# One top-p selection kernel: the repeat round is kept once per selection, and its ten halvings become a loop

## The chip, the core and the metric

The kernel is one program for one core of a Trainium2 chip. The metric is the device time of one execution in microseconds (us); lower is better. Three executions of the kernel before took 2766.83, 2774.76 and 2774.62 us, median 2774.62, mean 2772.07.

## The reference

The model is layer norm(x + G0), and then layer norm(x + G1) of that, on 3327 nodes with 128 features and a 3327 x 3327 adjacency matrix with values in 0.05 to 1 where there is an edge. G0 is a graph network with top-p ("nucleus") attention, in two steps:

```python
q = X @ W1.T @ W2.T ;  k = X @ W3.T
probs = softmax(q @ k.T)
idx = argsort(-probs) ; sp = take_along_axis(probs, idx) ; cs = cumsum(sp)
mask = ones where cs - sp < 0.9, at idx      # the largest until they hold 0.9 of the mass
A = probs * mask ; A = A / A.sum(-1)
# twice:  Xf = R @ Xf ; Xa = A @ Xa ; Z += Xf @ U1[n].T + Xa @ U2[n].T      R: adj + I, rows normalised
```

G1 has an edge part (a GRU cell on adj @ h, three graph attention heads with a masked softmax over every row) and a node part (a second GRU cell). The change concerns only G0, and in it only the step that decides which entries of a row of probabilities are kept.

## The kernel before

**Tiling.** 3327 rows are 26 tiles of 128 partitions, handled as 13 pairs (`PAIRS`). A row of logits or probabilities is 3328 wide and lies in a buffer `e`. `layer0` runs the two steps (step 0 and step 1), `normalize_and_sum` the norm and the sparse product, and a third function the attention heads (called layer 1 here).

**Who does what.** TensorE (PE) makes the logits (L819), the small transposes of flags (L861), the transposes of the kept probabilities (L925) with the products after them (L935), the adjacency product (L839) and the products `taken` (L879). ScalarE (ACT) copies and exponentiates, GpSimd (POOL) marks rows, SyncE (SP) issues the loads. VectorE (DVE) finds each row's largest values (L71), solves for the cut by halvings (the search, whose first instruction is L1304), and selects. The engines run streams of their own and meet at semaphores.

**The selection.** `Search.select` is placed twice for each pair, once for each of its two tiles `k`. Its inner function `divide` marks candidates of a tie at the cut (L439, a match-and-replace over the whole row), drops ties that exceed the mass (L444, the same kind of instruction), and keeps what is above the cut (L450). Between L439 and L444 stands an `If` (L480) on a register `kind`: where `kind` says OPEN, the search did not close the cut, and `another_round` narrows it. Between L444 and L450 stands a second `If` (L492) for more than 8 ties. Below, the part inside the first `If` is called the skipped body, since it is passed whenever `kind` is not OPEN.

**The skipped body.** It holds `another_round` twice: in `Fori(0, 3)` under an `If`, and in `while_over`, three nested loops of `Fori` and `If` (L80 to L86). Each `another_round` has ten halvings written out, one after another, each with a masked sum over the candidates of the round, a comparison with the wanted mass and a step up or down of the bit pattern `round_mid`. `while_over` places its body once, whatever its number of turns.

**Order of the work in step 1.** On DVE, `over_pairs_with_rows` is a loop of three turns with two pairs each (pairs 0 to 5), pair 6 written out, a loop of two turns (pairs 7 to 10), and pairs 11 and 12 written out; then comes `taken_batch`, one more tile with the rows that were taken out. A pair on DVE is: search of pair p, tops of pair p+1 for both tiles (L71), `assign_slots` (waits for PE's transposed flags), a wait for POOL, select of tile 0, select of tile 1. Each selection ends with a reciprocal (L1352) that lets PE start on that tile (L925). PE's loop is cut elsewhere, pairs 0 to 3 and 7 to 10; in a pair it does the transposes and products of both tiles, makes the logits two pairs ahead, and waits for the search of the next pair (L861). SP's `adj` loads run beside it, 1664 KB each. In step 0 a pair has no drops (L444) and no `adj` loads; a selection there first keeps (L450) and then passes the whole of `divide`, with the skipped body in it, by one jump, and the order is search, flags (L1340), select tile 0, tops, select tile 1, tops.

**What a text of the program does to an engine.** Each `select` is written out at each of its places in the instruction stream: a pair in a loop has two places, used by every turn. DVE has 21 selections placed; the skipped body stands in each.

Of the kernel before, what the change touches and what calls it, by code (L numbers as in the profile page):

```python
# [8 lines left out]
ALU = mybir.AluOpType  # L9
ACT = mybir.ActivationFunctionType  # L10
AX = mybir.AxisListType
# [7 lines left out]
ROUND_HALVINGS = 10  # L19
FINE_HALVINGS = 16  # L20
LOW_BITS = 0x37C00000
FIRST_STEP = 1 << 26
# [5 lines left out]
OPEN = 256  # L28
# [16 lines left out]
def spread_flags(eng, works):  # L45

    eng.drain()
    for w in works:
        eng.transpose(w["flags_t"][:, :], w["flags"][:, :])
    eng.drain()  # L50
    for w in works:
        eng.tensor_reduce(w["flag_max"][:, :], w["flags_t"][:, :], AX.X, ALU.max)
    eng.drain()
    for w in works:
        eng.tensor_copy(w["flag_int"][:, :], w["flag_max"][:, :])
    eng.drain()


def load_flag(eng, w, flag, regs):

    for q in range(4):
        eng.reg_load(regs[q], w["flag_int"][32 * q:32 * q + 1, 0:1])
    eng.reg_alu(flag, regs[0], regs[1], ALU.max)
    eng.reg_alu(flag, flag, regs[2], ALU.max)
    eng.reg_alu(flag, flag, regs[3], ALU.max)
# [8 lines left out]
def while_over(eng, flag, least, times, body):  # L74


    side = 1
    while side ** 3 < times:
        side += 1
    with eng.If(eng.snap(flag) > least):  # L80
        with eng.Fori(0, side):
            with eng.If(eng.snap(flag) > least):
                with eng.Fori(0, side):
                    with eng.If(eng.snap(flag) > least):
                        with eng.Fori(0, side):
                            with eng.If(eng.snap(flag) > least):  # L86
                                body()


class Search:  # L90
# [2 lines left out]
             "over", "up", "known", "reaches", "covers", "partial", "short", "strict", "backward", "cut_dropped", "scale", "levels", "shut", "mass_hi", "rowmax",  # L93
             "negmax", "open", "over_full", "spilled", "slot", "blank", "inv_kept0", "inv_kept1", "kept",
             "r_above0", "r_theta", "r_below", "r_was", "r_stays", "r_moves", "r_tau", "r_hi", "r_value", "r_bound",
             "r_above", "r_known", "r_up", "r_mass")

    def __init__(self, sb, width):
        self.width = width
# [32 lines left out]
    def one(self, name, k):  # L132
        return self.scalars[:, self.NAMES.index(name), k:k + 1]
# [194 lines left out]
    def another_round(self, eng, k, e):  # L328


        def one(name):
            return self.one(name, k)
# [18 lines left out]
        eng.memset(self.round_mid[:, :], LOW_BITS + FIRST_STEP)  # L351
        eng.drain()
        eng.tensor_tensor(one("r_stays"), one("r_stays"), one("known"), ALU.max)
        step = FIRST_STEP
        for n in range(ROUND_HALVINGS):
            eng.scalar_tensor_tensor(spare, cand, self.round_mid[:, :].bitcast(F32), cand, ALU.is_ge, ALU.mult,
                                     accum_out=self.mass[:, n, k:k + 1])
            back = -(step // 2) if n + 1 < ROUND_HALVINGS else 0
            eng.tensor_scalar(self.round_back[:, :], self.round_mid[:, :], float(back), None, ALU.add)
            eng.drain()  # L360
            eng.tensor_tensor(one("r_up"), self.mass[:, n, k:k + 1], one("r_theta"), ALU.is_ge)
            eng.drain()
            eng.scalar_tensor_tensor(self.round_mid[:, :], one("r_up"), float(step), self.round_back[:, :],
                                     ALU.mult, ALU.add)
            eng.drain()
            step //= 2
        eng.tensor_scalar(self.low[:, 0:ROUND_HALVINGS, k], self.mass[:, 0:ROUND_HALVINGS, k], one("r_theta"), None, ALU.is_lt)
        eng.drain()
        eng.tensor_tensor(self.low[:, 0:ROUND_HALVINGS, k], self.low[:, 0:ROUND_HALVINGS, k], self.mass[:, 0:ROUND_HALVINGS, k], ALU.mult)
        eng.drain()  # L370
        eng.tensor_reduce(one("r_hi"), self.low[:, 0:ROUND_HALVINGS, k], AX.X, ALU.max)
        eng.scalar_tensor_tensor(spare, cand, self.round_mid[:, :].bitcast(F32), cand, ALU.is_lt, ALU.mult)
        eng.drain()
        eng.max(top8, spare)
# [78 lines left out]
    def select(self, eng, k, e_pad, kind, flag, regs, both_ways, found=False):  # L453


        def another():
            self.another_round(eng, k, e_pad[:, 0:self.width])
            spread_flags(eng, [self.round])
            load_flag(eng, self.round, flag, regs)

        def more_ties():
            self.find_ties(eng, k)
            for n in range(TIES // 8):
                self.mark_ties(eng, k, n, self.work[:, :])
                eng.drain()
            self.pass_ties(eng, k)
            eng.tensor_scalar(self.one("r_up", k), self.one("left", k), 0.0, 4.0, ALU.is_gt, ALU.mult)
            eng.drain()
            eng.tensor_tensor(self.round["flags"][:, 0:1], self.one("r_up", k), self.one("strict", k), ALU.mult)
            spread_flags(eng, [self.round])  # L470
            load_flag(eng, self.round, flag, regs)

        def divide():
            if not found:
                if both_ways:
                    self.find_drops(eng, k)
                self.find_ties(eng, k)
            self.mark_ties(eng, k, 0, e_pad)
            eng.reg_mov(flag, kind)
            with eng.If(eng.snap(kind) > OPEN - 1):  # L480
                eng.drain()
                with eng.Fori(0, 3):
                    with eng.If(eng.snap(flag) > OPEN - 1):
                        another()
                while_over(eng, flag, OPEN - 1, self.width // 8, another)
                eng.drain()
                self.find_ties(eng, k)
                self.mark_ties(eng, k, 0, e_pad)
            eng.drain()
            if both_ways:  # L490
                self.drop_ties(eng, k)
            with eng.If(eng.snap(flag) > 1):  # L492
                eng.drain()
                self.mark_ties(eng, k, 1, self.work[:, :])
                with eng.If(eng.snap(flag) > 2):
                    eng.drain()
                    self.mark_ties(eng, k, 2, self.work[:, :])
                    eng.drain()
                    self.pass_ties(eng, k)
                    while_over(eng, flag, 3, self.width // TIES, more_ties)  # L500
                    eng.drain()
                eng.drain()
            eng.drain()
            self.keep(eng, k, e_pad, self.work)

        if both_ways:
            with eng.If(eng.snap(kind) > 0):
                divide()
            with eng.If(eng.snap(kind) < 1):
                self.keep(eng, k, e_pad, e_pad)  # L510
        else:
            with eng.If(eng.snap(kind) < 1):
                self.keep(eng, k, e_pad, e_pad)
            with eng.If(eng.snap(kind) > 0):
                divide()
        eng.drain()
# [1825 lines left out]
```

## Time and profile before

| | |
|---|---|
| span of the profiled execution | 2769.2 us |
| its own time | 2770.99 us |
| what lies outside the span | 1.8 us |
| runs | 2766.83, 2774.76, 2774.62 us |
| granted TensorE clock, mean | 0.934 of full speed |
| PE busy | 2355.1 us (85%), 17759 matmuls |
| DVE busy | 2199.7 us (79%), 6636 instructions |
| ACT busy | 1072.5 us (39%) |
| POOL busy | 141.5 us (5%) |

How to read it: busy time is summed over the whole span, in which stages with different limits follow each other. Step 0 of G0 is at about 67 to 510 us, step 1 at about 577 to 1458 us with `taken_batch` behind it, layer 1's attention from about 1600 us to the end. Idle time stands in brackets behind an instruction, with what ended it; "issue" is idle time in which the engine waited for nothing that the profile shows.

### The profile page before, as it was taken

Reading aid. Unit: us, or ns where it says so; the run is one execution under the profiler, and the core shown is the slowest. Engines: PE = TensorE matmul, PEld = TensorE weight load, DVE = VectorE, ACT = ScalarE, POOL = GpSimd, SP = SyncE. Lnnn points to the kernel's source line nnn. Section 1 sums busy time; section 2 is a strip of 40 time slices with the busy share of each in tenths; the row PEclk is TensorE's granted clock in tenths of the full one; section 3 lists DMA queues with packets and bytes.
Section 4 is the critical chain, followed back from the end, with each engine's and each line's share of the span. In section 5 each row is a group of like instructions: output and inputs, shape, how many; then the busy total and the mean of one; then the engine's idle time right before and its main releaser. Section 6 shows DMA issues by size and latency. Waiting matters only on the chain. (4 is left out here: it accounts for less than half of the span.)

```text
span 2769.2 us, 53551 instructions
## 1 busy us (share of the span) xinstructions
PE 2355.1 (85%) x17759; PEld 1987.9 (72%) x17759; DVE 2199.7 (79%) x6636; ACT 1072.5 (39%) x1785; POOL 141.5 (5%) x353
## 2 busy tenths in 40 slices
PE   5899998777888887888886649996999999999985
PEld 1566666555767776777775549995999999999952
DVE  2777777279888888888889777766999999999836
ACT  4566666433333333333333130003343443434423
POOL 0000000101111110000000010000000000000000
PEclk9999999997999998999997869998999999999997
DMA  3000000020222221222220235543334343433220
GB/s 128 2 2 1 1 1 2 1 89 17 95 100 100 100 100 51 100 100 101 100 100 14 87 128 202 202 164 127 126 108 143 101 146 104 141 110 134 94 88 25
DMA packets 57106, 245.00 MB, mean 88 GB/s; under 512 B 6705, under 2 KB 18352, under 8 KB 43120
## 3 DMA queue, kind: packets, MB, share of 16 engines
q1 hardware_dynamic: 56816, 241.94, 24.9%
q14 instruction: 207, 1.70, 0.2%
q8 instruction: 83, 1.36, 0.2%
HBM read 235.10 MB, written 6.82 MB: 87 GB/s over the span
## 5 line engine op out<-in xcount | busy, mean ns | idle before, releaser
L1932 PE MATMUL a_acc<-H,pT 128*128 128x128 f32 x4056 | 547.8, 277 | 11.7 <-ACT a_rows L1964 3.8
L1932 PEld LDWEIGHTS a_acc<-H,pT 128*128 128x128 f32 x4056 | 495.3, 192 | 28.7 <-DVE pT L2066 19.9
L935 PE MATMUL small<-XR,wT 128*128 128x128 f32 x2756 | 375.9, 282 | 28.3 <-ACT wT L1131 27.5
L71 DVE MAX8 cand<-e 128x8 f32<-128x64 f32 (+3 forms) x1898 | 302.7, 240 | 101.4 <-issue 101.2
L819 PE MATMUL lg<-kT,qs 128*128 128x512 f32 (+1 forms) x742 | 339.9, 596 | 50.5 <-ACT e L1075 38.5
L935 PEld LDWEIGHTS small<-XR,wT 128*128 128x128 f32 x2756 | 341.6, 196 | 44.4 <-ACT wT L1131 44.4
L2066 DVE TENSOR_TENSOR pT<-a_tr,a_adjT 128x512 f32<-128x512 f32 (+1 forms) x546 | 316.3, 643 | 22.5 <-PE a_tr L1891 19.3
L839 PE MATMUL accR<-XR,adj 128*128 128x129 f32 x2704 | 327.2, 283 | 0.0
L839 PEld LDWEIGHTS accR<-XR,adj 128*128 128x128 f32 x2704 | 324.1, 200 | 0.0
L1891 PE MATMUL a_tr<-ident,prob 128*128 128x128 f32 x2028 | 311.2, 274 | 10.9 <-ACTq L1958 10.9
L1131 ACT ACTIVATE wT<-tr 128x512 f32<-128x512 f32 (+1 forms) x371 | 206.2, 566 | 273.1 <-PE tr L925 271.4
L2044 DVE CUSTOM_DVE_ANT_0 prob<-a_adj,EB 128x3328 f32<-128x3328 f32 x78 | 282.6, 3623 | 0.0
L819 PEld LDWEIGHTS lg<-kT,qs 128*128 128x128 f32 x742 | 119.0, 193 | 216.9 <-ACT e L1075 168.6
L925 PE MATMUL tr<-ident,e 128*128 128x128 f32 x1378 | 213.2, 282 | 56.0 <-DVE scalars L1352 49.9
L1075 ACT ACTIVATE e<-lg 128x512 f32<-128x512 f32 (+1 forms) x371 | 206.3, 566 | 119.2 <-PE lg L819 117.3
L1891 PEld LDWEIGHTS a_tr<-ident,prob 128*128 128x128 f32 x2028 | 241.0, 142 | 11.1 <-issue 11.1
L1956 ACT ACTIVATE prob<-prob,a_negmax 128x3328 f32<-128x3328 f32 x78 | 239.0, 3064 | 9.1 <-DVE a_negmax L2053 9.1
L925 PEld LDWEIGHTS tr<-ident,e 128*128 128x128 f32 x1378 | 167.7, 146 | 95.7 <-DVE scalars L1352 51.6
L1580 PE MATMUL g_sp<-g_adj,H 128*128 128x128 f32 x1352 | 166.1, 286 | 17.1 <-ACTq L1645 17.1
L1580 PEld LDWEIGHTS g_sp<-g_adj,H 128*128 128x128 f32 x1352 | 161.9, 201 | 18.8 <-issue 18.2
L1085 ACT ACTIVATE e<-e,scalars 128x3327 f32<-128x3327 f32 x53 | 162.1, 3060 | 15.9 <-DVE scalars L1416 8.8
L219 DVE SCALAR_TENSOR_TENSOR work<-cand,mid 128x416 f32<-128x416 f32 (+1 forms) x198 | 143.2, 757 | 8.1
(334 smaller groups left out, 2457.1 us busy)
## 6 DMA issues: line engine op xcount, KB each, us to landing
adj<-in_adjT SPq DMA_DIRECT2D x52, 1664.0 KB, 7.3
g_adj<-in_adjT SPq DMA_DIRECT2D x26, 1664.0 KB, 6.9
a_adj<-in_adj SPq DMA_DIRECT2D x26, 1664.0 KB, 6.8
a_adjT<-in_adjT SPq DMA_DIRECT2D x156, 256.0 KB, 3.9
a_adjT<-in_adjT SPq DMA_DIRECT2D x26, 128.0 KB, 4.2
XT<-in_x_t SPq DMA_DIRECT2D x1, 1664.0 KB, 13.5
hT_scratch<-hT SPq DMA_DIRECT2D x1, 1664.0 KB, 12.2
nsT_scratch<-nsT SPq DMA_DIRECT2D x1, 1664.0 KB, 5.8
```

The source lines that it names most:

```text
L71: eng.max(cand[:, n, :], src[:, n * seg:min((n + 1) * seg, width)])
L819: eng.matmul(lg[bank][:, 0:sl.stop - sl.start], qs[k][:, :], kT[:, sl], start=True, stop=True).then_inc(lg_ready, 1)
L839: mm = eng.matmul(accR[:, :], adj[k][:, j * P:(j + 1) * P], xf[:, j, :], start=False, stop=(j == T - 1))
L925: mm = eng.transpose(tr[(k * NC + c) % 2][:, o:o + P], e[b][k][:, j * P:(j + 1) * P], ident[:, :])
L935: mm = eng.matmul(accA[:, :], wT[(k * NC + c - 1) % 2][:, o:o + P], xa[:, j, 0:P], start=(j == 0), stop=(j == T - 1))
L1075: eng.activation(e[b][k][:, sl], lg[chunk(step, 0, k, c) % 2][:, 0:sl.stop - sl.start], ACT.Copy).then_inc(lg_free, 1)
L1580: mm = eng.matmul(sp[k][:, :], H[:, j, :], adj[q][:, j * P:(j + 1) * P], start=(j == 0), stop=(j == T - 1))
L1891: mm = eng.transpose(tr[g % BANKS][:, (j % 4) * P:(j % 4 + 1) * P], prob[order[n][1]][:, j * P:(j + 1) * P], ident[:, :])
L1932: mm = eng.matmul(acc[:, :], pT[g % RING][:, (j % 4) * P:(j % 4 + 1) * P], H[:, j, :], start=(j == 0), stop=(j == T - 1))
L1956: eng.activation(prob[h][:, :], prob[h][:, :], ACT.Exp, bias=negmax[h][:, :], accum_out=den[h][:, :])
L2044: eng.tensor_tensor_reduce(prob[h][:, :], adj[k][:, :], EB[:, h, :], 1.0, -3.0e38, ALU.add, ALU.max, mx[h][:, :])
L2066: eng.tensor_tensor(pT[g % RING][:, 0:width(c)], tr[g % BANKS][:, 0:width(c)], adjT[:, c * 512:c * 512 + width(c)], ALU.mult).then_inc(pT_ ...
```

## The change

In `another_round` the ten halvings become `Fori(0, ROUND_HALVINGS)`. The step, a number of the program text before, is a value `r_step` that is halved in each turn, and the largest mass below the wanted one is kept as a running maximum `r_hi` instead of being taken from ten stored masses at the end; one addition behind the loop makes up for the last step. In `select` the `Fori(0, 3)` copy of the round goes, and only the one in `while_over` stays. While the three-turn loop and the nested loops both ran as long as the flag said OPEN, now the nested loops alone do.

```diff
--- before.py
+++ after.py
@@ -93,7 +93,7 @@
              "over", "up", "known", "reaches", "covers", "partial", "short", "strict", "backward", "cut_dropped", "scale", "levels", "shut", "mass_hi", "rowmax",
              "negmax", "open", "over_full", "spilled", "slot", "blank", "inv_kept0", "inv_kept1", "kept",
              "r_above0", "r_theta", "r_below", "r_was", "r_stays", "r_moves", "r_tau", "r_hi", "r_value", "r_bound",
-             "r_above", "r_known", "r_up", "r_mass")
+             "r_above", "r_known", "r_up", "r_mass", "r_step", "r_half", "r_low")
 
     def __init__(self, sb, width):
         self.width = width
@@ -351,24 +351,26 @@
         eng.memset(self.round_mid[:, :], LOW_BITS + FIRST_STEP)
         eng.drain()
         eng.tensor_tensor(one("r_stays"), one("r_stays"), one("known"), ALU.max)
-        step = FIRST_STEP
-        for n in range(ROUND_HALVINGS):
+        eng.memset(one("r_hi"), 0.0)
+        eng.memset(one("r_step"), float(FIRST_STEP))
+        eng.drain()
+        with eng.Fori(0, ROUND_HALVINGS):
             eng.scalar_tensor_tensor(spare, cand, self.round_mid[:, :].bitcast(F32), cand, ALU.is_ge, ALU.mult,
-                                     accum_out=self.mass[:, n, k:k + 1])
-            back = -(step // 2) if n + 1 < ROUND_HALVINGS else 0
-            eng.tensor_scalar(self.round_back[:, :], self.round_mid[:, :], float(back), None, ALU.add)
+                                     accum_out=one("r_mass"))
+            eng.tensor_scalar(one("r_half"), one("r_step"), 0.5, None, ALU.mult)
             eng.drain()
-            eng.tensor_tensor(one("r_up"), self.mass[:, n, k:k + 1], one("r_theta"), ALU.is_ge)
+            eng.tensor_tensor(one("r_up"), one("r_mass"), one("r_theta"), ALU.is_ge)
+            eng.scalar_tensor_tensor(one("r_low"), one("r_mass"), one("r_theta"), one("r_mass"), ALU.is_lt, ALU.mult)
+            eng.tensor_tensor(self.round_back[:, :], self.round_mid[:, :], one("r_half"), ALU.subtract)
             eng.drain()
-            eng.scalar_tensor_tensor(self.round_mid[:, :], one("r_up"), float(step), self.round_back[:, :],
+            eng.scalar_tensor_tensor(self.round_mid[:, :], one("r_up"), one("r_step"), self.round_back[:, :],
                                      ALU.mult, ALU.add)
+            eng.tensor_tensor(one("r_hi"), one("r_hi"), one("r_low"), ALU.max)
             eng.drain()
-            step //= 2
-        eng.tensor_scalar(self.low[:, 0:ROUND_HALVINGS, k], self.mass[:, 0:ROUND_HALVINGS, k], one("r_theta"), None, ALU.is_lt)
-        eng.drain()
-        eng.tensor_tensor(self.low[:, 0:ROUND_HALVINGS, k], self.low[:, 0:ROUND_HALVINGS, k], self.mass[:, 0:ROUND_HALVINGS, k], ALU.mult)
-        eng.drain()
-        eng.tensor_reduce(one("r_hi"), self.low[:, 0:ROUND_HALVINGS, k], AX.X, ALU.max)
+            eng.tensor_copy(one("r_step"), one("r_half"))
+            eng.drain()
+        eng.tensor_scalar(self.round_mid[:, :], self.round_mid[:, :], float(FIRST_STEP >> ROUND_HALVINGS), None, ALU.add)
+        eng.drain()
         eng.scalar_tensor_tensor(spare, cand, self.round_mid[:, :].bitcast(F32), cand, ALU.is_lt, ALU.mult)
         eng.drain()
         eng.max(top8, spare)
@@ -479,9 +481,6 @@
             eng.reg_mov(flag, kind)
             with eng.If(eng.snap(kind) > OPEN - 1):
                 eng.drain()
-                with eng.Fori(0, 3):
-                    with eng.If(eng.snap(flag) > OPEN - 1):
-                        another()
                 while_over(eng, flag, OPEN - 1, self.width // 8, another)
                 eng.drain()
                 self.find_ties(eng, k)
```

PE's, ACT's, POOL's and SP's streams keep every instruction and its order. DVE's stream gets shorter: 6869 rows before, 4286 after.

The first place is DVE's stream in the first selection of step 1, where the skipped body begins. `L439`/`L441` is the first mark of ties on the row `e`; the branches behind it are the `If` on `kind` and the loops; `L338` begins `another_round`. Before:

```order
L439 MATCH_REPLACE work<-hits,e 128x3336
L479 ISA
L480 COMPARE_AND_BRANCH
L482 UNCONDITIONAL_BRANCH
L483 COMPARE_AND_BRANCH
L338 SCALAR_TENSOR_TENSOR work,scalars<-e,scalars 128x3328
```

After:

```order
L441 MATCH_REPLACE work<-hits,e 128x3336
L481 ISA
L482 COMPARE_AND_BRANCH
L80 COMPARE_AND_BRANCH
L81 UNCONDITIONAL_BRANCH
L82 COMPARE_AND_BRANCH
L83 UNCONDITIONAL_BRANCH
L84 COMPARE_AND_BRANCH
L85 UNCONDITIONAL_BRANCH
L86 COMPARE_AND_BRANCH
L338 SCALAR_TENSOR_TENSOR work,scalars<-e,scalars 128x3328
```

Nothing ahead of the `If` has moved; behind it the first copy of the round is gone and the nested loops come at once.

The second place is inside `another_round` on DVE, the halvings on the candidates `round_cand`. One of ten halvings before:

```order
L356 SCALAR_TENSOR_TENSOR work,mass<-round_cand,round_mid 128x208
L359 TENSOR_SCALAR round_back<-round_mid 128x1
L361 TENSOR_TENSOR scalars<-mass,scalars 128x1
L363 SCALAR_TENSOR_TENSOR round_mid<-scalars,round_back 128x1
```

The whole loop after:

```order
L357 UNCONDITIONAL_BRANCH
L358 SCALAR_TENSOR_TENSOR work,scalars<-round_cand,round_mid 128x208
L360 TENSOR_SCALAR scalars<-scalars 128x1
L362 TENSOR_TENSOR scalars<-scalars 128x1
L363 SCALAR_TENSOR_TENSOR scalars<-scalars 128x1
L364 TENSOR_TENSOR round_back<-round_mid,scalars 128x1
L366 SCALAR_TENSOR_TENSOR round_mid<-scalars,round_back 128x1
L368 TENSOR_TENSOR scalars<-scalars 128x1
L370 COPY scalars<-scalars 128x1
L357 REGISTER_ALU
L357 COMPARE_AND_BRANCH
```

Forty instructions in each copy of the round have become eleven.

The third place is where DVE lands when the skipped body is passed, at the end of the same selection. Before:

```order
L421 TENSOR_SCALAR hits<-hits,scalars 128x24
L439 MATCH_REPLACE work<-hits,e 128x3336
L480 UNCONDITIONAL_BRANCH
L444 MATCH_REPLACE work<-drops,work 128x3336
L492 COMPARE_AND_BRANCH
```

After:

```order
L423 TENSOR_SCALAR hits<-hits,scalars 128x24
L441 MATCH_REPLACE work<-hits,e 128x3336
L482 UNCONDITIONAL_BRANCH
L446 MATCH_REPLACE work<-drops,work 128x3336
L491 COMPARE_AND_BRANCH
```

From the `If` (L480, L482 after) to its landing (L444, L446 after) there are 205 rows before and 82 after; counted in the built program, with drains and register moves, which the order does not list, 411 instructions before and 156 after. The second `If` (L492, L491 after) passes 70 built instructions in both.

## Rows read from the trace of the kernel before

**Rows 1.** Windows of step 0, step 1, layer 1: busy us (instructions), clock, DMA, GB/s

```profile
core 0: us, PE busy (x) PEld busy (x) DVE busy (x) ACT busy (x) POOL busy (x), PEclk, DMA share, GB/s
67.00:510.00 443.00, 390.14 (x2335) 281.33 (x2336) 341.61 (x1403) 275.08 (x461) 28.48 (x70) 0.98 0.01 2
577.00:1458.00 881.00, 749.26 (x5015) 618.72 (x5016) 752.03 (x3090) 323.12 (x547) 91.94 (x223) 0.92 0.25 91
1600.00:2769.00 1169.00, 1034.27 (x9456) 968.91 (x9456) 955.90 (x1520) 384.56 (x625) 7.39 (x2) 0.95 0.37 127
```

**Rows 2.** Waits of PE, 622 to 1490: total us, times, longest

```profile
PE tr L925 <- DVE scalars L1352: 26.4, 5, 11.6
...
PE small L861 <- DVEq L326: 15.0, 8, 3.1
PE taken L879 <- issue: 11.7, 9, 4.7
```

**Rows 3.** Waits of DVE, 577 to 1458: total us, times, longest

```profile
DVE work L444 <- issue: 28.2, 17, 2.6
...
DVE gate L1304 <- issue: 10.3, 3, 4.7
DVE e L450 <- issue: 6.0, 4, 2.1
DVE cand L71 <- issue: 4.7, 3, 2.9
```

**Rows 4.** Groups of DVE instructions, 577 to 1458: count, busy us, mean ns, idle

```profile
L439 DVE MATCH_REPLACE8 work<-hits,e 128x3336 f32<-128x3336 f32 x24 | 86.8, 3618 | 0.0
L444 DVE MATCH_REPLACE8 work<-drops,work 128x3336 f32<-128x3336 f32 x24 | 86.8, 3617 | 0.0
```

**Rows 5.** Timeline of DVE, third pair of step 1: start, us, idle before

```profile
764.02 3.62 DVE L439 MATCH_REPLACE8 work<-hits,e 128x3336 f32<-128x3336 f32 x1
...
770.23 0.09 DVE L444 MATCH_VALUE_LOAD work<-drops,work 128x8 f32 x1 [2.60 <-issue]
...
778.28 3.62 DVE L439 MATCH_REPLACE8 work<-hits,e 128x3336 f32<-128x3336 f32 x1
...
783.72 0.09 DVE L444 MATCH_VALUE_LOAD work<-drops,work 128x8 f32 x1 [1.82 <-issue]
```

**Rows 6.** Timeline of DVE, last pair of step 1

```profile
1458.64 3.62 DVE L439 MATCH_REPLACE8 work<-hits,e 128x3336 f32<-128x3336 f32 x1
1462.33 0.09 DVE L444 MATCH_VALUE_LOAD work<-drops,work 128x8 f32 x1
```

**Rows 7.** Timeline of DVE, one selection of step 0

```profile
222.73 0.41 DVE L1340 TENSOR_REDUCE pair_flag_int<-small 1x2 int32<-1x256 f32 x1 [1.52 <-PE small L861]
224.07 3.69 DVE L450 SCALAR_TENSOR_TENSOR e<-e,scalars 128x3328 f32<-128x3328 f32 x1 [0.93 <-issue]
...
227.84 0.16 DVE L1352 RECIPROCAL scalars<-scalars 128x1 f32<-128x1 f32 x1
```

**Rows 8.** Timeline of PE in step 1, its waits for DVE and for instructions

```profile
788.10 1.23 PE L879 MATMUL taken<-XR,XT 128*128 x4 [4.67 <-issue]
...
1066.61 1.97 PE L925 MATMUL tr<-ident,e 128*128 128x128 f32 x8 [10.98 <-DVE scalars L1352]
...
1219.46 1.09 PE L925 MATMUL tr<-ident,e 128*128 128x128 f32 x8 [1.47 <-DVE scalars L1352]
...
1246.56 0.38 PE L861 MATMUL small<-ident,pair_flags 128*1 128x128 f32 x2 [3.09 <-DVEq L326]
...
1289.67 1.23 PE L879 MATMUL taken<-XR,XT 128*128 x4 [4.68 <-issue]
...
1578.63 1.97 PE L925 MATMUL tr<-ident,e 128*128 128x128 f32 x8 [13.86 <-DVE scalars L1352]
```

**Rows 9.** DMA queues, 711 to 1433: packets, MB, share of 16 engines

```profile
q8 instruction: 38, 0.62, 0.3%
q14 instruction: 86, 0.70, 0.3%
```

**Rows 10.** DMA queues, 2030 to 2590: the only one

```profile
q1 hardware_dynamic: 25820, 69.30, 36.7%
```

## The prediction

> **What bounds the kernel now.** I read first the windows [rows 1]. In step 0 PE is busy 390.1 of 443 us, DVE 341.6; in step 1 both are near each other, PE 749.3 and DVE 752.0 of 881 us; in layer 1 PE has 1034.3 of 1169. So only in step 1 can time taken off DVE reach the end, and there only where PE waits for it. Then the groups of DVE in step 1 [rows 4]: L439 on `e` has run 24 times and L444 24 times, two for each of the twelve pairs that begin their selections in the window, and no instruction of `another_round` (L338 to L414) has a row. The changed lines never execute with these inputs. What the change does to the time it does by the length of DVE's instruction stream, or not at all.
>
> That the length matters is to be seen in the waits of DVE [rows 3]. Ahead of L444 DVE was idle 28.2 us in 17 of 24 cases, up to 2.6 us, and no semaphore or transfer ended it. L444 is the landing of the `If` that passes the skipped body. Ahead of L450, the landing of the second `If`, it is 6.0 us in 4 cases. The timeline of the third pair [rows 5] shows one closely: L439 begins at 764.02 and is over at 767.64, L444 begins at 770.23, 2.60 later; in the next tile 1.82. The stall is even longer than it looks, since DVE's sequencer could go for the landing while L439 was still running its 3.62 us. In the last pair [rows 6] the same place costs nothing: 1458.64 plus 3.62 is 1462.26, and L444 follows at 1462.33. I read the stall as the fetch of the text at the landing. The trace has two queues of kind "instruction", and in the 722 us from 711 to 1433 they brought 86 packets with 0.70 MB and 38 with 0.62 MB [rows 9].
>
> The Trainium skill ("Runtime: NRT & Kernel Launch", Instruction fetch mechanics) says that a taken branch to a target outside the two blocks held makes the engine fetch before it goes on, blocks being 16 KiB or 256 instructions. The trace agrees in part: one queue has 0.62 MB in 38 packets, 16.3 KB each, but the other 0.70 MB in 86, 8.2 KB each [rows 9]. By that page's block a jump over 411 instructions misses nearly always and one over 156 often stays inside; by half that block, as the 8.2 KB would have it (128 instructions), 156 is still beyond one block and sometimes beyond the next. What the first would give is weighed among the rivals.
>
> **The change part by part.** *Step 0.* A selection keeps (L450, 3.69 us) and then jumps over all of `divide`. L450 begins at 224.07 and the reciprocal behind it at 227.84 [rows 7], so the jump lies under the 3.69 us, and before it DVE waited 1.52 us for PE's flags. Bounds 0 and the few stalls of 0.93; DVE waits for PE in each pair, so I take 0.
>
> *Step 1, the first jump.* The price now is 28.2 / 24 = 1.18 us for a jump over 411 built instructions. The second jump passes 70 and costs 6.0 / 24 = 0.25 [rows 3, 4]. The new first jump passes 156. Nothing in the trace passes 156, so its price has the ends 0 (all saved: 28.2, and 6.0 more if the second jump's misses go with it: 34.2 us) and 1.18 (nothing saved: 0). On a straight line between the two rows it is 0.25 + 0.93 x (156 - 70) / (411 - 70) = 0.25 + 0.23 = 0.48 us. That saves 0.70 us for each selection, 24 x 0.70 = 16.8 us of DVE time in step 1. I take this since both ends of the line are measured on this engine in this stage. The second jump stays at 0.25.
>
> *What of it reaches the end.* The waits of PE [rows 2] have 26.4 us for L1352, of which 11.6 are at the start of the stage, and 15.0 for the search's flags (L861). Along the timeline [rows 8] the large one is 10.98 us at 1066.61, in pair 6, the one where PE's order of work turns: PE is ready for the transposes and waits for the selection. It ends 13 selections after the start, 13 x 0.70 = 9.1 us, all below 10.98, so the whole 9.1 passes. Five selections on, at 1246.56, DVE has 18 x 0.70 = 12.6; the 3.5 more are covered by PE's waits of 1.47 (1219.46) and 3.09 (1246.56), together 4.56. For the last six (4.2 us) DVE begins to wait for PE's logits instead (L71, 4.7 us in 3 cases, [rows 3]), so of these nothing more comes. Behind the stage the chain goes through `taken_batch` on DVE (PE waits 13.86 us at 1578.63), which moves with the rest. The sum is 12.6; with half a microsecond off for what DVE loses already ahead of pair 6 in waiting for PE, 12 us. Its ends: nothing, and, with all stalls gone, the sum of PE's waits from pair 6 on, 10.98 + 1.47 + 3.09 + about 1 = 16.5 us, behind which PE paces alone.
>
> *What stays.* The back edges of DVE's loop (L1304, 10.3 us in 3 cases [rows 3]) jump back over two pairs, far further than either jump even when the text is shorter, and PE's own fetches of 4.67 and 4.68 us [rows 8] are PE's. The halvings as a loop, eleven instructions where forty stood, would cost more per turn if they ran; they don't, so 0.
>
> *The sum.* The profiled execution took 2770.99 us, its span 2769.2 and 1.8 around it. 2771.0 - 12 = 2759.0. The runs' mean is 2772.1 and their median 2774.6, which give 2760.1 and 2762.6. I predict 2760.
>
> **The rivals.**
> *All stalls of the jumps go.* The body passed becomes so short that the landing is always at hand. For it: 70 instructions miss in only 4 cases of 24, and the last pair has none. Against it: those 4 cases, for a shorter jump than the new one. DVE saves 34.2 us, of which 16.5 pass: 2771.5 - 16.5 = 2755. The Trainium skill's rule (the same section), with its block of 256 instructions, comes near this.
>
> *Nothing changes.* 156 instructions are still beyond what DVE holds when it jumps, and one fetch is needed either way: 2.60 us idle behind a 3.62 us instruction [rows 5] looks like one fetch of a fixed time. For it: the stall has sizes near each other (up to 2.6, and 2.1 at the second jump) whatever the distance passed, and at the second jump the distance is 70. Against it: misses at 70 are 4, at 411 they are 17. DVE saves under 2 us, and the time is 2771 to 2775.
>
> *Slower.* The text of DVE from step 1 on lies elsewhere than before: all of it moves. Layer 1's attention loop now runs without a single packet of instructions in 560 us [rows 10], so its text fits in what DVE holds. If, moved, it straddles one piece more than is held, each of its 11 turns (a pair of tiles each, the first and the last pair written out) fetches at the back edge. A back edge costs 10.3 / 3 = 3.4 us on DVE [rows 3], 11 x 3.4 = 38 us, and DVE has 955.9 of 1169 us there beside PE's 1034.3 [rows 1]; where all of it passes, the time is 2759 + 38 = 2797. It decides from a third of that, 12 us, upward. For it: where the pieces of text begin relative to the loop changes with every instruction taken out ahead of it. Against it: nothing in the stretch shows that it is near the limit now.
>
> **How the numbers follow.** The forecast (-12) has a chance of 0.42, all stalls gone (-16.5) 0.22, nothing changed 0.29, slower 0.07. A difference of 0.3%, 8.3 us, is about what a measurement of this kernel can tell from none. Faster by more: 0.42 and 0.22, less 0.04 for a forecast that comes out at 8 us or less, 0.60. Within 0.3%: 0.29 and that rest, 0.33. Slower: 0.07. The range: down, 16.5 off the lowest run 2766.8 would be 2750, and 2748 with 2 for the unknown price of waits ended early; up, nothing changed on the median, 2774.6, and about one more, 2776. Outside are the slower case and the edges, about 0.15. The time I give is that of the likeliest case, 2760.
>
> **What would show it.** DVE's idle time ahead of L446 (L444 before) falls from 28.2 to about 11.5 us, with 17 cases becoming about 8; ahead of L452 it stays near 6.0. If it is under 2 the first rival is right, if over 24 the second. PE's wait at the transposes of pair 6, now 10.98, becomes about 2 (about 0 in the first rival, 11 in the second). Step 1's stretch from the first search to `taken_batch` gets 12 us shorter, step 0 and layer 1 keep their lengths. Packets of instructions in 2030 to 2590, none now, would show the slower case. The prediction is wrong if DVE's idle time goes as said and the end does not move, which would mean that PE has another wait right behind each; or if DVE's saving shows in step 0, where I have none.

## The result and the profile after

The changed kernel takes 2758.47 us (median of 5 runs, 2754.57 to 2759.01), the kernel before 2772.56 on the same chip; the ratio is 0.995, 95% interval 0.9934 to 0.9965. That is 14 us less. I had forecast 2760 and 12 us less. The profiled execution took 2758.67 us with a span of 2756.9, 12.3 us under the span before.

First, the waits of DVE in the same stretch, 577 to 1458 us (total us, times, longest), to be set beside [rows 3]. L446, L452 and L1303 are L444, L450 and L1304 of before:

```profile
DVE gate L1303 <- issue: 12.2, 3, 5.7
DVE work L446 <- issue: 12.2, 6, 2.6
DVE cand L71 <- issue: 10.9, 5, 5.1
...
DVE e L452 <- issue: 0.9, 2, 0.4
```

Ahead of the drop of ties 28.2 us have become 12.2, and ahead of the keep 6.0 have become 0.9. The tops (L71) wait 10.9 in place of 4.7: DVE arrives there before PE's logits. The timeline of DVE in the third pair of step 1, to be set beside [rows 5]:

```profile
763.72 3.62 DVE L441 MATCH_REPLACE8 work<-hits,e 128x3336 f32<-128x3336 f32 x1
769.89 0.09 DVE L446 MATCH_VALUE_LOAD work<-drops,work 128x8 f32 x1 [2.56 <-issue]
...
777.94 3.62 DVE L441 MATCH_REPLACE8 work<-hits,e 128x3336 f32<-128x3336 f32 x1
781.63 0.09 DVE L446 MATCH_VALUE_LOAD work<-drops,work 128x8 f32 x1
```

Tile 0 stalls as before, 2.56 us, and tile 1 no longer does. The price of this stall is the same (2.60 before); there are fewer of them. The DMA queues of instructions, 711 to 1433 (packets, MB, share), beside [rows 9]:

```profile
q8 instruction: 39, 0.64, 0.4%
q14 instruction: 71, 0.58, 0.2%
```

q14 brings 71 packets in place of 86, q8 as many as before, so q14 is the queue of DVE's text. PE's two waits, beside [rows 8]:

```profile
1059.99 1.97 PE L924 MATMUL tr<-ident,e 128*128 128x128 f32 x8 [9.54 <-DVE scalars L1351]
...
1567.53 1.97 PE L924 MATMUL tr<-ident,e 128*128 128x128 f32 x8 [13.86 <-DVE scalars L1351]
```

The first ends 6.6 us earlier, the second 11.1. Of these, 1.25 us are there already when step 1's search begins (L163 at 576.72, 577.97 before).

### The profile page after: what moved, and what is told of

The parts are those of the page before. It is cut to its first block and busy times, and to the rows that moved or that the text cites. A ratio compares the mean times of both kernels' runs of the same rounds, so it can differ in the third digit from the quotient of the medians.

```text
span 2756.9 us, 53551 instructions
## 1 busy us (share of the span) xinstructions
PE 2349.6 (85%) x17759; PEld 1984.4 (72%) x17759; DVE 2201.8 (80%) x6636; ACT 1071.8 (39%) x1785; POOL 139.2 (5%) x353
## 5 line engine op out<-in xcount | busy, mean ns | idle before, releaser
L1931 PE MATMUL a_acc<-H,pT 128*128 128x128 f32 x4056 | 549.1, 277 | 11.5 <-ACT a_rows L1963 3.7
L71 DVE MAX8 cand<-e 128x8 f32<-128x64 f32 (+3 forms) x1898 | 302.7, 240 | 105.3 <-issue 105.3
L1890 PE MATMUL a_tr<-ident,prob 128*128 128x128 f32 x2028 | 312.2, 274 | 10.9 <-ACTq L1957 10.9
L1890 PEld LDWEIGHTS a_tr<-ident,prob 128*128 128x128 f32 x2028 | 242.1, 142 | 11.1 <-issue 11.1
L1579 PE MATMUL g_sp<-g_adj,H 128*128 128x128 f32 x1352 | 159.2, 279 | 17.1 <-ACTq L1644 17.1
L1579 PEld LDWEIGHTS g_sp<-g_adj,H 128*128 128x128 f32 x1352 | 155.1, 194 | 18.9 <-issue 18.9
```

What stands on the lines that cost most here:

```text
L71: eng.max(cand[:, n, :], src[:, n * seg:min((n + 1) * seg, width)])
L1579: mm = eng.matmul(sp[k][:, :], H[:, j, :], adj[q][:, j * P:(j + 1) * P], start=(j == 0), stop=(j == T - 1))
L1890: mm = eng.transpose(tr[g % BANKS][:, (j % 4) * P:(j % 4 + 1) * P], prob[order[n][1]][:, j * P:(j + 1) * P], ident[:, :])
L1931: mm = eng.matmul(acc[:, :], pT[g % RING][:, (j % 4) * P:(j % 4 + 1) * P], H[:, j, :], start=(j == 0), stop=(j == T - 1))
```

## The experiments

Theory A: a jump costs a fetch where its landing lies outside the text that DVE holds, and the fetch shows where its packet comes later than the instruction that covers it. Theory B: the price goes by the distance, along the straight line on which my sum was made. A distance is the number of built instructions that the jump passes, and an instruction that is later split counts as one: 383 before and 151 after, which are the 411 and 156 of the finer count ahead. All times are medians, and each ratio is against the kernel before on the same chip; "stalls" is the idle time ahead of the drop of ties in 577 to 1458 us.

### How far the jump goes

One copy alone taken away, halvings as before:

```diff
-                with eng.Fori(0, 3):
-                    with eng.If(eng.snap(flag) > OPEN - 1):
-                        another()
                 while_over(eng, flag, OPEN - 1, self.width // 8, another)
```

> Only the three-turn copy of the round goes; the ten halvings stay written out. The jump passes 205 built instructions (383 before, 151 with both edits, split instructions taken as one). Theory A, held text: a landing costs a fetch when it lies outside the text that DVE holds, some 8 KB packets (about 128 instructions); 205 is mostly outside, so at least 18 of 24 landings fetch, and the idle time ahead of the drop of ties is 18 to 26 us in 577 to 1458; the time is 1 to 8 us under the kernel before. Theory B, straight line in the distance: 0.25 us at 70, 1.18 at 411, so about 0.6 for each, 15 us in all; the time is 8 to 12 us under before.

The loop of halvings alone, with both copies kept (in the changed kernel):

```diff
+                with eng.Fori(0, 3):
+                    with eng.If(eng.snap(flag) > OPEN - 1):
+                        another()
                 while_over(eng, flag, OPEN - 1, self.width // 8, another)
```

> Only the ten halvings become a loop; both copies of the round stay. The jump passes 275 built instructions. Theory A, held text: every landing is outside, so the idle time ahead of the drop of ties stays near 28 us (24 to 30) and the time within 4 us of the kernel before. Theory B, straight line: 0.8 us for each, 19 us in all, the time 5 to 8 us under before.

The three lines of the first copy placed three times in the kernel before:

> The kernel before with the three-turn copy of the round placed three times, so that the first jump passes 739 built instructions in place of 383. Theory A: the landing was always outside what is held and still is, one fetch; the idle time ahead of the drop of ties stays at 24 to 32 us and the time within 5 us of before. Theory B, straight line in the distance: 2.1 us for each of 24, 51 us, and the time 10 us and more above before.

And no round at all (the `while_over` line taken from the changed kernel, which leaves the repeat round out):

> The repeat round is left out altogether (it never runs with these inputs); the first jump passes 10 built instructions. Both theories: idle time ahead of the drop of ties under 2 us. If DVE's saving passes only as far as PE waits for it, the time is 14 to 18 us under before, hardly less than the changed kernel, and DVE waits more for PE's logits (over 10.9 us at the tops). If DVE alone paced step 1, it would be 30 us and more under before.

Measured, in the order of the distance. The time of before is that beside loop only, one copy and no round; it was 2773.35 beside longer and 2772.56 beside changed:

| passed | kernel | stalls, cases | time | ratio to before, 95% |
|---|---|---|---|---|
| 739 | longer | 35.6, 18 | 2773.48 | 1.0003, 0.9993 to 1.0012 |
| 383 | before | 28.2, 17 | 2771.39 | |
| 275 | loop only | 31.4, 17 | 2767.79 | 0.9983, 0.9968 to 0.9998 |
| 205 | one copy | 28.0, 14 | 2766.01 | 0.9981, 0.9972 to 0.999 |
| 151 | changed | 12.2, 6 | 2758.47 | 0.995, 0.9934 to 0.9965 |
| 10 | no round | none | 2751.53 | 0.9928, 0.9914 to 0.9942 |

The waits of DVE in three of these, one line of each. Longer:

```profile
DVE work L444 <- issue: 35.6, 18, 2.8
```

One copy:

```profile
DVE work L444 <- issue: 28.0, 14, 3.3
```

No round, where the drop has no line and the tops have:

```profile
DVE cand L71 <- issue: 14.7, 7, 5.8
```

Theory B falls. It wanted 15 us of stalls for 205 instructions and 51 for 739. From 205 up the sum is 28 to 36 us, and it drops between 205 and 151. The stalls of the longer kernel are a little above the 24 to 32 that I had given it, its time is that of before. Each edit alone gives a quarter to two fifths of the gain, 5.4 us for one copy less and 3.6 for the loop; only both together bring many landings within reach. In the one-copy kernel the sum ahead of the drop is that of before (I had expected 18 to 26, in at least 18 cases; it was 14), and what went is the 6.0 us ahead of the keep. The 3.6 us of the loop alone (0.6 to 8.9 by its interval) are not explained: its stalls ahead of drop and keep are those of before (31.4 + 2.7 against 28.2 + 6.0), its profiled execution is one of the long ones (2774.72), and its step 1, from the first search (L163) to PE's last wait for a selection, is 1005.4 us long, that of before 1000.7. Its runs spread from 2757.93 to 2778.0 us; the two shortest had a mean granted TensorE clock of 0.938 and 0.939, the longest 0.933, and no run says which of the two follows from the other.

### Where the text lies

```diff
+                    if step == 1:
+                        with eng.If(eng.snap(kinds[0]) > 1000):
+                            for _ in range(64):
+                                eng.memset(gate[:, :], 0.0)
                     tops(0, 0, 0)
```

> The changed kernel with 64 memsets that never run, behind an If ahead of step 1 on DVE, so that all later text of DVE lies about 66 instructions further on; every jump has its old length. Theory A: which landings miss depends on where pieces of text begin, so the stalls sit at other selections than in the changed kernel (there: tile 0 of pairs 1, 2, 4, 5 and 11, tile 0 of pair 0 a little), the sum is between 5 and 25 us, and the time may be off the changed kernel's by up to 8 us either way. Theory B, distance alone: the same selections stall, 12.2 us in all, and the time is within 2 us of the changed kernel's.

> As the shift by 64, with 32 memsets that never run. Theory A: again other selections stall than in the changed kernel or with 64; the time is off the changed kernel's by up to 8 us. Theory B: the same selections, the same time within 2 us.

Shifted by 64, the kernel takes 2755.88 us (0.9936, 0.9922 to 0.995); by 32, 2760.59 (0.9956, 0.9941 to 0.9971). Every jump is as long as in the changed kernel, yet the stalls have other sums and places. By 64: 5.1 us in 4 cases, at pairs 7 and 9. By 32: 3.8 in 2, at tile 1 of pairs 1 and 3. In the changed kernel they are at tile 0 of pairs 0, 1, 2, 4 and 5 and at tile 1 of pair 11 (where my expectation says tile 0). So distance alone does not decide a landing; the place where a piece of text begins does too. The packets of q14 from the start of the mark to the keep agree: at tile 0 of pair 1 two in the changed kernel and one when shifted by 64, at tile 1 of pair 9 one and two. Nor does this sum alone decide the time: with 3.8 us of stalls the shift by 32 is 12.8 us under before, the changed kernel with 12.2 is 14.1 under. Waits of DVE, shifted by 64:

```profile
DVE work L446 <- issue: 5.1, 4, 2.2
```

### What makes a fetch late

The loads of `adj` in the loop, in place of the whole rows:

```diff
-                            eng.dma_start(adj[k][:, :], d["adjT"][bass.ds((q * 2 + k) * P, P), :])
+                            eng.dma_start(adj[k][:, 0:P], d["adjT"][bass.ds((q * 2 + k) * P, P), 0:P])
```

> The kernel before with only the first pair of adj loads whole; all later ones of G0 bring 128 of the 3328 columns (64 KB in place of 1664 KB), so that the product with adj uses old values. The text and its jumps are untouched. Theory A1, a landing's packet is late because bulk loads are in its way: the packets of instructions are as many as before (86 in 711 to 1433), but come about 1 us after the mark starts in place of 3.5 to 4.3, under the mark's 3.62 us, and the idle time ahead of the drop of ties falls from 28.2 to under 4 us. Theory A2, a fetch takes its time whatever else runs: it stays over 24 us.

> The changed kernel with the same small adj loads (old values in the product). Theory A1: the idle time ahead of the drop of ties, 12.2 us in the changed kernel, is under 2, and the change is worth under 4 us against the kernel before with small loads. Theory A2: it stays near 12 us and the change keeps its worth of 12 to 15 us.

With small loads the kernel before takes 2749.68 us and the changed one 2749.91 (one run each), where 2769.55 is the median of before on that chip: the change is worth nothing that single runs can tell. From the first search to PE's last wait for a selection, the two take 981.0 and 983.0 us, the kernel before 1000.7 with whole loads. No drop of ties waits in either. PE's own waits for `adj` loads (7.8 us in 577 to 1490 before) are gone too, so not all of the 20 us under before need be stalls of DVE. The text still comes, in as many packets. DMA queues, 711 to 1433, of the kernel before with small loads:

```profile
q1 hardware_dynamic: 5472, 2.49, 1.2%
q8 instruction: 39, 0.64, 0.4%
q14 instruction: 85, 0.70, 0.3%
```

When they come is to be seen in short windows of the same view, at the first selection of the third pair. In the kernel before its mark starts at 764.02 [rows 5]; from 764.1 to 767.6, while it runs:

```profile
q1 hardware_dynamic: 96, 1.28, 90.4%
```

and from 767.6 to 770.2, up to the drop:

```profile
q1 hardware_dynamic: 39, 0.31, 34.7%
q14 instruction: 1, 0.01, 0.7%
```

With small loads the mark starts at 760.00 and the drop at 763.69, behind its 3.62 us without a gap; from 760.1 to 761.6:

```profile
q1 hardware_dynamic: 136, 0.06, 14.0%
q14 instruction: 1, 0.01, 2.1%
```

The packet for the landing comes within 1.6 us of the mark's start where the DMA engines are free, and more than 3.6 us after it where an `adj` load of 1664 KB keeps them 90% busy. The idle time is what the mark's 3.62 us don't cover. Back edges of DVE's loops (L1304), which nothing covers, show the whole price of a fetch: 2.80, 2.83 and 2.88 us with small loads, 2.80, 4.68 and 2.81 in the kernel before. So a fetch that meets no bulk load fits under the mark. The small loads also sort the changed kernel's landings. Third pair, tile 0, 760.9 to 765:

```profile
q1 hardware_dynamic: 144, 0.07, 5.4%
q14 instruction: 2, 0.02, 1.3%
```

tile 1, 772.7 to 777:

```profile
q1 hardware_dynamic: 144, 0.07, 5.2%
q8 instruction: 1, 0.02, 1.8%
q14 instruction: 1, 0.01, 0.8%
```

In the 4 us from the start of the mark, every selection of the kernel before has two packets of q14 or more. In the changed one only tile 0 of pairs 0 to 5, tile 1 of pair 11 and tile 0 of pair 12 have them; the others have one. The stalls of the changed kernel with whole loads are at this very list, less pairs 3 and 12. I read the pair of packets as a landing not held. Pair 3 fits as well: with whole loads no `adj` packet moves while the mark of its tile 0 runs (833.7 to 837.2), and it doesn't stall; at tile 0 of pair 5, which stalls for 2.06 us, `adj` keeps the DMA engines 98.7% busy (975.9 to 979.4). The Trainium skill ("Runtime: NRT & Kernel Launch", Instruction fetch mechanics) says that a taken branch out of the window held forces a fetch; the trace agrees (28.2 us of idle time in 17 cases). Its block of 256 instructions in 16 KiB is not what DVE's queue shows, 8.2 KB in each packet, and a jump over 205 still stalled 14 times.

An estimate, with blocks of half that size (128 instructions, as 8.2 KB is half of 16 KiB) of which DVE holds the present one and the next: a jump over d instructions from place x of its block lands outside where x + d is 256 or more, so from (d - 128) / 128 of the places, and from all when d is 256 or more. Of 24 jumps that is none for 115, 4 for 151, 14 for 205 and all for 383. Measured are none stalled at 115 (the short round, below), 7 not held at 151, at least 14 at 205, and 24 not held at 383. Two blocks of 256 would give none at 205 and 12 at 383. That DVE holds two blocks is inferred from these counts; no run shows it directly.

### A shorter round, and a round out of the way

```diff
-ROUND_SEG = 128
+ROUND_SEG = 512
...
-                while_over(eng, flag, OPEN - 1, self.width // 8, another)
+                with eng.Fori(0, self.width // 8):
+                    with eng.If(eng.snap(flag) > OPEN - 1):
+                        another()
```

> The changed kernel with the skipped body made shorter still: one loop of 416 turns in place of three nested ones of eight, and the round takes its tops from segments of 512 in place of 128. The first jump passes 115 built instructions (151 in the changed kernel). Theory A, held text in pieces of about 128 instructions with the next one at hand: a jump of less than one piece lands in the present or the next one, so the idle time ahead of the drop of ties falls from 12.2 us to under 5, and the time is 16 to 20 us under the kernel before. Theory B, straight line in the distance: 0.25 + 0.93 x 45/341 = 0.37 us for each, 9 us in all, the time 13 to 16 us under before.

> The changed kernel once more, beside the one with the short round on the same chip. Theory A: 12 to 16 us under before, idle time ahead of the drop of ties near 12 us in the same selections as in its first profile.

> The kernel with the short round once more, on the same chip as the changed one. Theory A, stalls of the jumps gone and PE pacing the rest: 2 to 8 us under the changed kernel. If the stalls left in the changed kernel were covered anyway, the two are within 2 us.

The short round takes 2754.0 us (0.9933, 0.9919 to 0.9946), and no drop waits. Run again beside the changed kernel it takes 2752.22 (0.993, 0.9917 to 0.9944) against 2759.7 (0.9959, 0.9942 to 0.9975), 7.5 us less. It is the best version here that keeps the round. The second profile of the changed kernel has 7.6 us of stalls in 5 cases, the first 12.2 in 6, at the same selections less one: whether an unheld landing shows depends on whether an `adj` load is under way then. Its 9.9 us under before miss the 12 to 16 that I had expected, so the change is worth 10 to 14 us on two chips. Waits of DVE, short round:

```profile
DVE cand L71 <- issue: 13.4, 6, 5.7
DVE gate L1305 <- issue: 12.7, 4, 6.2
```

The other way, in the changed kernel:

```diff
+                        with eng.If(eng.snap(flag) < OPEN):
+                            select(p, b, 0, False)        # no round in it
+                            select(p, b, 1, False)
+                        eng.reg_alu(flag, kinds[0], kinds[1], ALU.max)
+                        with eng.If(eng.snap(flag) > OPEN - 1):
                             select(p, b, 0)
                             select(p, b, 1)
```

> The changed kernel, with the selection twice: both tiles of a pair without any round first, where neither needs one, and behind it, passed by one jump for each pair, both tiles with the round as changed. No long jump is left between the mark and the drop of ties; the one jump comes behind the release of the second tile. Theory A: idle time ahead of the drop under 2 us; one fetch for each pair, 12 of them at 0 to 2.6 us, ahead of the reciprocal of row sums or the next search; the back edges of DVE's loops stay. Time 12 to 18 us under before, so within 4 us of the changed kernel on either side. Rival: the text of a pair grows, the back edges and the jump together take back what the landings gave, and the time is 5 us or more above the changed kernel's.

It takes 2796.22 us (1.0082, 1.0069 to 1.0095), 25 us above before and some 38 above the changed kernel: the rival, and with 38 us in place of the 5 and more that it named. Timeline of DVE around one end of a pair:

```profile
867.58 0.16 DVE L1352 RECIPROCAL scalars<-scalars 128x1 f32<-128x1 f32 x1
871.10 0.16 DVE L1357 RECIPROCAL inv_sums<-rawR 128x1 f32 x1 [3.36 <-issue]
875.87 0.59 DVE L1357 RECIPROCAL inv_sums<-rawR 128x1 f32 x3 [4.61 <-issue]
879.37 0.06 DVE L1304 MEMSET gate<- 128x1 f32 x1 [2.92 <-issue]
```

and its waits in the whole stretch:

```profile
DVE inv_sums L1357 <- issue: 34.2, 10, 5.2
DVE gate L1304 <- issue: 26.9, 7, 6.4
```

The drops are free (0.9 us), but behind the selections there is no instruction of 3.62 us to cover a fetch. The jump's landing, a further piece of text a few short instructions on, and the back edge each wait in full, 10.9 us together here; that the middle one is a further piece of text is my reading of a packet of q14 that comes there (871 to 875.8). I had priced the single jump at 0 to 2.6 us; that is the price under a cover.

## Why the prediction was right

**What bounds it, and that the round never runs.** Right. With no round at all (every instruction that runs is still there) the kernel is 20 us faster; the gain comes from what is jumped over.

**The price of the new jump.** 0.48 us was forecast for each, 11.5 us in all; 12.2 were measured, in 6 cases where I said about 8. The number is right and its line is not: the line gives 15 us for 205 and 51 for 739, where 28.0 and 35.6 were measured. That it came out near at 151 is luck. A landing costs nothing or up to 2.6 us here, and 0.48 is a mean over both. The rival of a landing still outside is what tile 0 of the first pairs shows; it was true of 7 of 24, of which 6 stalled. The prediction had the right mechanism at hand, "by half that block, ... 156 is still beyond one block and sometimes beyond the next", and did not count it out: 28 of 128 places, 5 of 24. It did not count out the whole block either: two blocks of 256, as the Trainium skill ("Runtime: NRT & Kernel Launch", Instruction fetch mechanics) has them, let a jump over 411 miss from 155 of 256 places, not "nearly always", and one over 156 from none.

**The second jump.** Mis-sized: I left it at 6.0 us, 0.9 remain. DVE saved 21 us ahead of drops and keeps, not 16.8. In the kernel before each of the four stalls ahead of a keep stands behind a stall at the drop of the same selection, and with small loads both are gone. So I read them as fetches that follow a late one; no run sets them apart. The reading of rows was off too: 3 of the 24 selections enter the second `If` (a second mark, L439 on `work`, stands between their drop and their keep), so its price was 6.0 / 21 = 0.29 us and the same line gives 0.51 for the new jump and 16.0 us saved.

**What passes to the end.** 12 us forecast. From the first search (L163) to PE's last wait for a selection the profile before has 1578.63 - 577.97 = 1000.7 us, after 1567.53 - 576.72 = 990.8, so 9.8 us (8.3 in the second profile of the changed kernel). The path was not the one I gave. At pair 6 PE's wait ends 5.4 us earlier within the step, not 9.1, and the wait is still 9.54 us, not 2: PE itself arrives there 3.9 us earlier within the step. Two of its waits for the search's flags (1.29 and 1.57 us) are gone and two others have grown, 0.9 us less in all; where the other 3 us come from is not shown. DVE is ahead by most at the search of pair 10: 1291.51 before, 1275.73 after, 15.8 us, of which 14.5 within the step. Then PE paces, as forecast, but takes back more: 14.5 us there are 9.8 at the end. So the 12 us are right in part by luck, since DVE saved more than forecast and more of it was lost. Timeline of DVE, the tops of pairs 11 and 12:

```profile
1305.03 0.22 DVE L71 MAX8 cand<-e 128x8 f32<-128x64 f32 x1 [5.10 <-issue]
...
1375.19 0.22 DVE L71 MAX8 cand<-e 128x8 f32<-128x64 f32 x1 [4.01 <-issue]
```

These are 9.1 us where 4.5 had been. The remaining 2.5 us of the span's 12.3 lie outside step 1; the same kernel's step 1 began 1.6 us later in its second profile, so they are no effect that I can claim.

**The most that there is.** I had put all stalls gone at 16.5 us, by adding up PE's waits from pair 6 on. Without a round it is 20, with the short round 17 to 19, and small loads give about as much. The sum began at pair 6 and left out that PE gets there earlier as well, by 3.9 us. The same span of the step is 982.5 us with the short round (1560.20 - 577.70), 18.2 less than before (15.8 in its second profile).

**The slower case.** It did not come: from 2030 to 2590 the changed kernel has one packet on each queue of text, against one for each of some ten turns if the loop had not fitted. None of the kernels with moved text showed it.

## What to carry to other kernels

Text that never runs can cost time where a hot loop jumps over it. Look for "issue" idle time at the first instruction behind an `If`, and keep what it passes short enough to land in text already held (here a jump over 115 instructions between the mark and the drop never stalled, one over 151 did in a quarter of the cases, over 205 in more than half). Keep such a jump right behind the issue of a long instruction: moved to where only short ones run, a single jump for each pair cost more than the two it replaced.

## What I had not expected of the hardware

Bulk loads set the price of a missed landing. The same packet of 8.2 KB came within 1.6 us of the mark's start with the DMA engines free and after more than 3.6 us beside a load of 1664 KB, and of the 10 to 14 us that the change is worth nothing is seen when these loads are 64 KB (2749.68 against 2749.91 us, one run each). A saving on one engine also shifts its jumps against the loads, so how much of the stalls is left varies by run: 12.2 and 7.6 us in two profiles of one kernel.
